# Queries, r and k of five steps as three products of high and low parts, with the buffers and the element-wise work that go with them

## The chip, the core and the metric

The kernel runs on one core of a Trainium2 chip. The metric is device time in microseconds (us). Before the change three runs gave 287.93, 290.63 and 290.19 us, so the median is 290.19 us.

## What is computed

The input is x of shape 4 x 1024 x 256, all in float32. Two blocks follow each other, each behind a layer norm and with a residual.

```
a = layernorm(x)
q = a Wq + bq            k = (a Wk + bk) Wc We      v = (a Wv + bv) Wc We      16 heads of 16, 4 key heads
o = causal linear attention with features elu + 1, divided by (q . cumsum k + 1e-6)
x2 = x + layernorm(a + o Wo + bo) * gamma + beta
z = layernorm(x2),  z_prev = z one token earlier
r = sigmoid((mu_r z + (1 - mu_r) z_prev) Wr^T)
k = relu((mu_k z + (1 - mu_k) z_prev) Wk^T)^2
out = x2 + r * (k Wv^T)
```

## The kernel before, in words

The 1024 tokens are cut into 8 chunks of 128. A chunk holds the 4 batches side by side: 512 columns, in two halves of channels. The kernel has no planner. Each of the five engines has its own program, an order written out by hand, and semaphores join them.

The programs are software-pipelined over steps c = 0 to 6 and a finale. A step works on four chunks at once: it finishes the attention of chunk c, prepares chunk n = c + 1 (transposed input aT, keys, values, queries, denominators), applies output projection and layer norm to chunk m = c - 1, and runs the FFN of chunk f = c - 2. Steps 0 and 1 have no FFN (step 1 has m only), steps 2 to 6 have all four, and the finale (c = 7) runs the attention of the last chunk and the FFN of chunks 5, 6 and 7.

The order in a step with an FFN, engine by engine:

- **TensorE (PE)**: transpose z of f (L469), transpose a of n (L368), spread the reciprocals (L415), output projection (L461), scores (L432), keys and values (L375), r of f (`mix_r`, L483), attention outputs (L448, L453), queries of n (`queries`, L381), keys transposed (L389), state increments (L398), scores, k of f (`mix_k`, L476), outputs, denominators (L406), outputs, v of f (`mix_v_parts`, L501 and L505), first scores of n. L381, L476 and L483 take float32 operands. `mix_v_parts` already uses parts: the product A B is A_high B_high + A_high B_low + A_low B_high, where high is a copy in the type float32r and low is the rest. It holds three matmuls where `mix_v` (L491, the finale) holds one of float32.
- **VectorE (DVE)**: mask of scores (L991), statistics of x (L917), two token shifts for r (L1051, xr), residual of m (L1016) with its statistics, mask, keys and values (L939, L940), centring of m (L1026), key features (L944, L947), second residual of m (L1037, it makes x2), division (L1005), mask, first queries (L953), two token shifts for k (L1051, xk), second queries, division, states (L968), running key sums (L962), statistics of x2, mask, division, two low parts of k's activation (L1109), reciprocal, division, two gates (L1064).
- **ScalarE (ACT)**: copies of zT, aT and the reciprocals, `normalise_x` (L777), exponentials of the keys, tanh of r (L812), exponentials of the queries (L731, L733), copies of values and states, relu, square and high copy of k (L801, L803, L711), copies of transposed keys, `normalise_z` (L785). All copies go through a helper on L711.
- **GpSimd (POOL)**: two token differences (L271, dz), scale and bias of the next x (L222, L216, L218, L226), a + bo (L248), 1/sigma of m (L216, L218), x + beta (L255), denominator terms (L263, prod), scale and bias of z (L222 to L226), two output sums (L278).

The prediction gives places in a step relative to S, the start of the z transposes on TensorE (L469). In the step that is shown S is at 137.57 us.

## Time and profile before

| | |
|---|---|
| median of the runs | 290.19 us |
| profiled execution, whole | 290.58 us |
| its span | 288.8 us |
| busy PE / DVE / ACT / POOL | 264.8 / 225.1 / 154.1 / 127.3 us |
| granted TensorE clock, mean | 0.976 of full |
| step with an FFN, S to S | 30.80 us |
| steps 0 and 1 with the start (to S of step 2) | 74.2 us |
| five steps with an FFN | about 156 us |
| finale | about 58 us |

A row of the timeline has the start in us, the time from the first start to the last end of the merged instructions, the engine, the line, the operation, and the count. A bracket at its end has the idle time before it and what ended that. TensorE's share of busy time is the highest, and a step with an FFN shows hardly a gap on it. The other engines show theirs in brackets.

### The profile page before, as it was taken

Reading aid. Unit: us, or ns where it says so; the run is one execution under the profiler, and the core shown is the slowest. Engines: PE = TensorE matmul, PEld = TensorE weight load, DVE = VectorE, ACT = ScalarE, POOL = GpSimd, SP = SyncE. Lnnn points to the kernel's source line nnn. Section 1 sums busy time; section 2 is a strip of 40 time slices with the busy share of each in tenths; the row PEclk is TensorE's granted clock in tenths of the full one; section 3 lists DMA queues with packets and bytes.
Section 4 is the critical chain, followed back from the end, with each engine's and each line's share of the span. In section 5 each row is a group of like instructions: output and inputs, shape, how many; then the busy total and the mean of one; then the engine's idle time right before and its main releaser. Section 6 shows DMA issues by size and latency. Waiting matters only on the chain.

```text
span 288.8 us, 7520 instructions
## 1 busy us (share of the span) xinstructions
PE 264.8 (92%) x2961; PEld 190.6 (66%) x2961; DVE 225.1 (78%) x550; ACT 154.1 (53%) x312; POOL 127.3 (44%) x151
## 2 busy tenths in 40 slices
PE   7886988983899999999999999999999999989794
PEld 6755656742685588757885588558855767766563
DVE  6587487969597979977997989796979758977523
ACT  2384684480643866388456854586248630453540
POOL 2628423100983358515853576355543514051510
PEclk9998999996599999999999999999999999999999
DMA  7900120000020003000400020001000020000312
GB/s 195 265 19 11 65 76 3 2 0 2 4 72 0 2 24 123 2 5 2 145 2 2 0 76 2 0 2 64 13 2 3 1 74 2 0 2 1 109 36 73
DMA packets 12178, 10.73 MB, mean 37 GB/s; under 512 B 2288, under 2 KB 12144, under 8 KB 12144
## 3 DMA queue, kind: packets, MB, share of 16 engines
q1 hardware_dynamic: 11392, 9.97, 11.1%
q8 instruction: 23, 0.38, 0.5%
q10 hardware_dynamic: 752, 0.30, 0.4%
q14 instruction: 11, 0.09, 0.1%
HBM read 6.07 MB, written 4.19 MB: 36 GB/s over the span
## 4 chain that ended last, share of the span: by engine, by line
PE 77%; DVE 11%; ACT 5%; issue 3%; DMA 2%; POOL 1%; ACTq 0%; DVEq 0%; POOLq 0%
PE ps_x L461 10%; PE ps_x L381 9%; PE ps_z L432 6%; PE ps_x L476 6%; PE ps_x L483 6%; PE ps_x L375 6%; PE ps_y L448 5%; PE ps_y L453 5%; PE ps_x L501 4%; PE ps_x L469 3%; PE ps_z L476 3%; PE ps_z L483 2%; DVE probs L991 2%; PE ps_x L368 2%; PE ps_z L415 2%
## 5 line engine op out<-in xcount | busy, mean ns | idle before, releaser
L991 DVE TENSOR_TENSOR probs<-ps_z,causal 128x1024 f32<-128x1024 f32 x32 | 38.7, 1211 | 6.3 <-PE ps_z L432 5.5
L461 PE MATMUL ps_x<-wo_sb,oT 128*128 128x256 f32 x128 | 29.6, 382 | 0.0
L381 PE MATMUL ps_x<-aT,wq_sb 128*128 128x512 f32 x60 | 27.8, 604 | 0.0
L278 POOL TENSOR_TENSOR out_tok<-tanh_r,x_tok 128x512 f32<-128x512 f32 x14 | 17.8, 1275 | 21.9 <-DVE tanh_r L1064 20.9
L461 PEld LDWEIGHTS ps_x<-wo_sb,oT 128*128 128x128 f32 x128 | 23.6, 190 | 3.8 <-issue 0.9
L248 POOL TENSOR_TENSOR abo_tok<-a_tok,bo_bc 128x1024 f32<-128x1024 f32 x8 | 18.9, 2361 | 16.3 <-issue 5.6
L255 POOL TENSOR_TENSOR xb_tok<-x_in,beta_bc 128x1024 f32<-128x1024 f32 x8 | 18.9, 2356 | 16.0 <-DVE x_tok L1037 16.0
L218 POOL TENSOR_TENSOR rstd<-rstd,neg_half 128x4 f32<-128x4 f32 x24 | 24.9, 1038 | 1.9
L448 PE MATMUL ps_y<-qf,state 32*32 32x128 f32 x512 | 20.9, 278 | 5.3 <-DVE oT L1005 4.7
L432 PE MATMUL ps_z<-qf,kfT 32*128 32x128 f32 x512 | 24.1, 304 | 1.4 <-ACT rden_bc L711 0.5
L263 POOL TENSOR_TENSOR prod<-qf,ksum 128x1024 f32<-128x1024 f32 x5 | 11.8, 2361 | 29.9 <-DVE ksum L962 29.9
L448 PEld LDWEIGHTS ps_y<-qf,state 32*32 32x32 f32 x512 | 12.1, 106 | 19.4 <-issue 11.7
L953 DVE SCALAR_TENSOR_TENSOR qf<-ps_x,bq,eq 128x512 f32<-128x512 f32 x15 | 11.2, 748 | 15.0 <-ACT eq L733 15.0
L432 PEld LDWEIGHTS ps_z<-qf,kfT 32*128 32x128 f32 x512 | 17.9, 191 | 7.4 <-issue 5.0
L222 POOL TENSOR_TENSOR neg_mean<-mv,neg_one 128x4 f32<-128x4 f32 x16 | 5.0, 312 | 38.7 <-DVE mv L923 38.7
L785 ACT ACTIVATE z_tok<-x_tok,nbias,rstd 128x256 f32<-128x256 f32 x32 | 16.6, 591 | 10.2 <-POOL nbias L226 10.2
L1064 DVE SCALAR_TENSOR_TENSOR tanh_r<-tanh_r,ps_x 128x512 f32<-128x512 f32 x13 | 8.9, 686 | 16.5 <-PE ps_x L491 6.5
L453 PE MATMUL ps_y<-probs,v_pad 128*32 128x128 f32 x512 | 21.1, 283 | 0.0
L731 ACT ACTIVATE eq<-ps_x,neg_bq 128x512 f32<-128x512 f32 x15 | 10.3, 687 | 19.9 <-PE ps_x L381 19.9
L777 ACT ACTIVATE a_tok<-x_in,nbias,rstd 128x256 f32<-128x256 f32 x24 | 12.4, 589 | 11.7 <-issue 11.7
L476 PE MATMUL ps_x<-xk,wkT 128*128 128x512 f32 x40 | 18.5, 605 | 0.0
L381 PEld LDWEIGHTS ps_x<-aT,wq_sb 128*128 128x128 f32 x60 | 10.8, 190 | 11.4 <-issue 10.5
(144 smaller groups left out, 623.6 us busy)
## 6 DMA issues: line engine op xcount, KB each, us to landing
x_in<-in_L_attn_x_dram SPq DMA_DIRECT2D x8, 512.0 KB, 4.2
out_dram<-out_tok SPq DMA_DIRECT2D x16, 256.0 KB, 2.1
xr<-in_L_attn_Wq_dram ACTq DMA_DIRECT2D x1, 256.0 KB, 4.0
xk<-in_L_ffn_W_r_dram SPq DMA_DIRECT2D x1, 256.0 KB, 4.8
xk<-in_L_ffn_W_k_dram SPq DMA_DIRECT2D x1, 256.0 KB, 5.0
xr<-in_L_ffn_W_v_dram SPq DMA_DIRECT2D x1, 256.0 KB, 5.5
wo_sb<-in_L_attn_Wo_dram SPq DMA_DIRECT2D x4, 64.0 KB, 5.0
bo_bc<-in_L_attn_bo_dram SPq DMA_DIRECT2D x1, 128.0 KB, 5.0
```

What stands on the lines that cost most here:

```text
L218: PL.tensor_tensor(dst[:], dst[:], neg_half[:], ALU.pow).then_inc(done, 1)
L248: PL.tensor_tensor(abo_tok[n % 2][:], a_tok[n % 2][:], bo_bc[:].unsqueeze(1).to_broadcast([P, NB, D]), ALU.add).then_inc(s_ab, 1)
L255: PL.tensor_tensor(xb_tok[n % 2][:], x_in[n % XBUF][:], beta_bc[:].unsqueeze(1).to_broadcast([P, NB, D]), ALU.add).then_inc(s_xb, 1)
L278: PL.tensor_tensor(out_tok[:, 2 * i:2 * i + 2, :], tanh_r[:, i].rearrange("p (b d) -> p b d", b=2), x2_tok[m % 3][:, 2 * i:2 * i + 2, :], ...
L381: last = mm(bk_[:, :], wq_sb[:, k, a, :], aT[:, k, :], start=(k == 0), stop=(k == KD - 1))
L432: last = mm(ps_z[:, g, u * P:(u + 1) * P], kfT[c % 2][rows, 2 * b + u, :, :], qf[c % 2][rows, :, t0:t0 + HALF], start=True, stop=True, ski ...
L448: mm(ps_y[rows, off + u * P:off + (u + 1) * P], state[rows, slot, b, :, :], qf[c % 2][rows, :, t0:t0 + HALF], start=(u == 0), stop=False, ...
L453: last = mm(ps_y[32 * g:32 * g + 32, off + u * P:off + (u + 1) * P], v_pad[c % 2][:, b, u, g, :, :], probs[b % 2][:, g, u * P:(u + 1) * P] ...
L461: last = mm(bk_[:, (b % 2) * D:(b % 2 + 1) * D], oT[m % 2][:, a, b, :], wo_sb[:, a, :], start=(a == 0), stop=(a == 1))
L476: last = mm(bk_[:, :], wkT[:, k, n * P:(n + 1) * P], xk[:, k, :, :], start=(k == 0), stop=(k == KD - 1))
L483: last = mm(bk_[:, (b % 2) * D:(b % 2 + 1) * D], xr[:, k, b, :], wrT[:, k, :], start=(k == 0), stop=(k == KD - 1))
L991: V.tensor_tensor(probs[b % 2][:].rearrange("p g (r s) -> p g r s", s=HALF), ps_z[:, :, 0:2 * P].rearrange("p g (r s) -> p g r s", s=HALF) ...
```

## The change

**Three products instead of float32.** In steps 2 to 6 the queries, r and k are computed from parts as v already was (`query_parts`, `mix_r_parts`, `mix_k_parts`). In the finale r and v are too, and k stays float32. High parts are copies on ScalarE, low parts are subtractions on GpSimd, both 128x512: six of each in a step, for xr, aT and xk. xr and xk share one pair of buffers, `shift_high` and `shift_low`. The weights Wq, Wr and Wk are split once, in step 0.

**Buffers shared.** z_tok lies in a_tok, prod in eq, wrT and wvT in y_tok. This brings waits with it.

**The shorter steps.** In step 1 the centring and second residual of chunk 0 go from VectorE to ScalarE (`normalise_y`, four of 128x256) and GpSimd (`scale_residual`, eight of 128x256). The denominator terms of steps 0 and 1 go from VectorE to GpSimd, and TensorE takes the denominators behind the last outputs there.

**Order.** In steps 2 to 6 VectorE shifts for k before the first queries. In the finale VectorE makes the second residual of the last chunk behind the shifts for r of the one before it, and GpSimd makes three pairs of low parts for r and three for v.

The program of GpSimd for one step with an FFN (c = 3), first as it was (`dz` to `out_tok`; `mv` and `rstd` are those of x, of y and of z in this order):

```order
L271 TENSOR_TENSOR dz<-zT 128x512 x2
L222 TENSOR_TENSOR neg_mean<-mv,neg_one 128x4
L226 TENSOR_TENSOR nbias<-neg_mean,rstd 128x4
L248 TENSOR_TENSOR abo_tok<-a_tok,bo_bc 128x1024
L216 TENSOR_TENSOR rstd<-mv,ln_eps 128x4
L218 TENSOR_TENSOR rstd<-rstd,neg_half 128x4
L255 TENSOR_TENSOR xb_tok<-x_in,beta_bc 128x1024
L263 TENSOR_TENSOR prod<-qf,ksum 128x1024
```

and as it is with the change (where the denominator terms are written into `eq`):

```order
L292 TENSOR_TENSOR dz<-zT 128x512 x2
L233 TENSOR_TENSOR neg_mean<-mv,neg_one 128x4
L237 TENSOR_TENSOR nbias<-neg_mean,rstd 128x4
L305 TENSOR_TENSOR shift_low<-xr,shift_high 128x512 x2
L227 TENSOR_TENSOR rstd<-mv,ln_eps 128x4
L229 TENSOR_TENSOR rstd<-rstd,neg_half 128x4
L269 TENSOR_TENSOR abo_tok<-a_tok,bo_bc 128x1024
L305 TENSOR_TENSOR aT_low<-aT,aT_high 128x512 x2
L276 TENSOR_TENSOR xb_tok<-x_in,beta_bc 128x1024
L305 TENSOR_TENSOR shift_low<-xk,shift_high 128x512 x2
L284 TENSOR_TENSOR eq<-qf,ksum 128x1024
```

Six subtractions came in, and a + bo went behind 1/sigma of m. The sum x + beta, as before, needs x2 from VectorE.

ScalarE around the queries of the same step, with the change. The first `eq<-ps_x,neg_bq` is the first half of the queries, and `k_act` is the FFN's k:

```order
L831 ACTIVATE eq<-ps_x,neg_bq 128x512 [waits den_ps,qf_ready,q_ps]
L833 ACTIVATE eq<-eq 128x512 [waits negq]
L810 ACTIVATE shift_high<-xk 128x512 [waits xk_ready,r_ps]
L831 ACTIVATE eq<-ps_x,neg_bq 128x512 [waits den_ps,qf_ready,q_ps]
L833 ACTIVATE eq<-eq 128x512 [waits negq]
L810 ACTIVATE shift_high<-xk 128x512 [waits xk_ready]
L810 ACTIVATE v_pad<-v_half 64x4x4x16 [waits o_ps,kv_ready]
L810 ACTIVATE v_pad<-v_half 64x4x4x16 x3
L810 ACTIVATE state<-tail,row_mask 128x4x16 [waits tail_ready]
L810 ACTIVATE state<-tail,row_mask 128x4x16 x3
L908 ACTIVATE k_act<-ps_x 128x512 [waits v_ps,k_ps]
```

The two `shift_high` copies are new here, each of them ahead of work of the queries or the values, and each waits for a token shift of VectorE.

The core of the diff:

```diff
+            def low_parts(parts, whole, high, value, done):
+                for k in range(KD):
+                    pool.wait_ge(high, value + k + 1)
+                    PL.tensor_tensor(flat(parts[1])[:, k * T:(k + 1) * T], whole(k),
+                                     flat(parts[0])[:, k * T:(k + 1) * T].bitcast(F32), ALU.subtract).then_inc(done, 1)
...
+            def query_parts(n, a, bk_):
+                pe.wait_ge(s_aTh, 2 * n - 4)
+                for k in range(KD):
+                    for part in range(2):
+                        mm(bk_[:, :], wq_p[part][:, k, a, :], aT_p[0][:, k, :], start=(k == 0 and part == 0), stop=False)
+                pe.wait_ge(s_aTl, 2 * n - 4)
+                for k in range(KD):
+                    last = mm(bk_[:, :], wq_p[0][:, k, a, :], aT_p[1][:, k, :], start=False, stop=(k == KD - 1))
+                last.then_inc(s_q_ps, 1)
...
             def finale(c):
                 m, f = c - 1, c - 2
                 token_difference(f)
                 first_norm(m)
+                pool.wait_ge(s_k_ps, 2 * f)
+                low_xr(f)
                 second_norm(m)
+                low_ka(f)
                 first_norm(c)
                 token_difference(m)
+                low_xr(m)
                 second_norm(c)
+                low_ka(m)
                 finish(f)
+                low_xr(c)
                 finish(m)
+                low_ka(c)
...
+            def high_part(parts, whole, ready, value, done, ks=range(KD)):
+                for k in ks:
+                    act.wait_ge(ready, value + k + 1)
+                    copy(flat(parts[0])[:, k * T:(k + 1) * T], whole(k)).then_inc(done, 1)
...
                 divide(c, 0)
                 mask(c, 2)
-                queries(n, 0, x0)
                 token_shift(f, 0, *for_k)
                 token_shift(f, 1, *for_k)
+                queries(n, 0, x0)
                 queries(n, 1, x1)
...
                 queries(n, 0, x0)
+                if m >= 0:
+                    second_stats(m, (0, 1))
                 queries(n, 1, x1)
                 divide(c, 1)
                 states(n)
                 key_sums(n)
-                denominator_terms(n)
                 mask(c, 3)
-                if m >= 0:
-                    centre(m)
-                    second_residual(m)
                 divide(c, 2)
```

## Rows read from the trace of the kernel before

**Rows 1.** Busy by stretch of time: PE, PEld, DVE, ACT, POOL, PEclk, DMA share, GB/s.
```profile
65.50:70.00 4.50, 0.62 (x16) 0.35 (x16) 4.50 (x11) 0.00 (x0) 0.00 (x0) 0.75 0.01 4
70.00:78.20 8.20, 7.20 (x77) 5.09 (x77) 5.96 (x22) 3.85 (x8) 6.28 (x7) 0.51 0.00 0
137.57:168.70 31.13, 31.01 (x371) 22.41 (x368) 27.20 (x68) 19.38 (x39) 17.14 (x19) 1.00 0.11 35
```

**Rows 2.** Timeline of PE in one step with an FFN.
```profile
137.57 1.09 PE L469 MATMUL ps_x<-ident,z_tok 128*128 128x128 f32 x8
146.36 3.62 PE L483 MATMUL ps_x<-wrT,xr 128*128 128x256 f32 x16
151.71 3.70 PE L381 MATMUL ps_x<-aT,wq_sb 128*128 128x512 f32 x8
158.11 3.70 PE L476 MATMUL ps_x<-xk,wkT 128*128 128x512 f32 x8
164.65 0.39 PE L501 MATMUL ps_x<-wv_high,ka_high 128*128 128x256 f32 x1
...
167.72 0.73 PE L432 MATMUL ps_z<-qf,kfT 32*128 32x128 f32 x16
168.37 1.09 PE L469 MATMUL ps_x<-ident,z_tok 128*128 128x128 f32 x8
```

**Rows 3.** Timeline of POOL in the same step, and its one subtraction of this form.
```profile
139.33 2.04 POOL L271 TENSOR_TENSOR dz<-zT 128x512 f32<-128x512 f32 x2 [0.19 <-ACT zT L711]
141.32 0.65 POOL L222 TENSOR_TENSOR neg_mean<-mv,neg_one 128x4 f32<-128x4 f32 x1
143.81 0.20 POOL L226 TENSOR_TENSOR nbias<-neg_mean,rstd 128x4 f32<-128x4 f32 x1
144.75 2.37 POOL L248 TENSOR_TENSOR abo_tok<-a_tok,bo_bc 128x1024 f32<-128x1024 f32 x1 [0.75 <-ACT a_tok L777]
147.36 1.02 POOL L218 TENSOR_TENSOR rstd<-rstd,neg_half 128x4 f32<-128x4 f32 x1
151.57 2.35 POOL L255 TENSOR_TENSOR xb_tok<-x_in,beta_bc 128x1024 f32<-128x1024 f32 x1 [3.19 <-DVE x_tok L1037]
...
43.44 1.27 POOL L303 TENSOR_TENSOR wv_low<-wvT,wv_high 128x512 fp32r<-128x512 f32 x1 [5.63 <-ACT wv_high L711]
```

**Rows 4.** Timeline of DVE in the same step.
```profile
140.71 1.87 DVE L1051 SCALAR_TENSOR_TENSOR xr<-dz,mu_r_col,zT 128x512 f32<-128x512 f32 x2
147.50 1.66 DVE L1026 SCALAR_TENSOR_TENSOR y_tok<-y_tok,mv,gamma_bc 128x256 f32<-128x256 f32 x4
149.82 1.67 DVE L1037 SCALAR_TENSOR_TENSOR x_tok<-y_tok,rstd,xb_tok 128x256 f32<-128x256 f32 x4
155.11 0.75 DVE L953 SCALAR_TENSOR_TENSOR qf<-ps_x,bq,eq 128x512 f32<-128x512 f32 x1 [1.92 <-ACT eq L733]
155.78 1.41 DVE L1051 SCALAR_TENSOR_TENSOR xk<-dz,mu_k_col,zT 128x512 f32<-128x512 f32 x2
```

**Rows 5.** Timeline of ACT in the same step.
```profile
153.73 0.69 ACT L731 ACTIVATE eq<-ps_x,neg_bq 128x512 f32<-128x512 f32 x1 [2.89 <-PE ps_x L381]
161.43 0.63 ACT L711 ACTIVATE ka_high<-k_act 128x512 fp32r<-128x512 f32 x1
```

**Rows 6.** Durations of the shifts for r by line, ns min/median/max, in the whole run.
```profile
L1051 DVE SCALAR_TENSOR_TENSOR xr<-dz,mu_r_col,zT x16: 737/743/1511, 79.1 to 275.2; 128x512 f32<-128x512 f32 x16
```

**Rows 7.** Timeline of PE and DVE in step 1.
```profile
66.38 1.66 DVE L1026 SCALAR_TENSOR_TENSOR y_tok<-y_tok,mv,gamma_bc 128x256 f32<-128x256 f32 x4
70.02 1.08 PE L448 MATMUL ps_y<-qf,state 32*32 32x128 f32 x16 [3.90 <-DVE oT L1005]
```

**Rows 8.** Timeline of POOL and PE in the finale.
```profile
253.59 0.20 POOL L226 TENSOR_TENSOR nbias<-neg_mean,rstd 128x4 f32<-128x4 f32 x1
267.12 0.20 POOL L226 TENSOR_TENSOR nbias<-neg_mean,rstd 128x4 f32<-128x4 f32 x1
269.13 1.04 PE L469 MATMUL ps_x<-ident,z_tok 128*128 128x128 f32 x8
```

More of the change, by code:

```diff
@@ L103, in build @@
         s_kd = sem("kf_doubled")
+        wq_p, wr_p, wk_p = ([ctx.enter_context(nc.sbuf_tensor(f"{name}_{part}", [P, *shape], F32R)) for part in ("high", "low")]
+                               for name, shape in (("wq", (KD, 2, P)), ("wr", (KD, D)), ("wk", (KD, D))))
+        wq_split, wr_split, wk_split = sem("wq_split"), sem("wr_split"), sem("wk_split")
+        aT_p, shift_p = ([ctx.enter_context(nc.sbuf_tensor(f"{name}_{part}", [P, KD, T], F32R)) for part in ("high", "low")]
+                         for name in ("aT", "shift"))
+        xr_p = xk_p = shift_p
+        s_aTh, s_aTl, s_xrh, s_xrl, s_xkh, s_xkl = (
+            sem("aT_high"), sem("aT_low"), sem("xr_high"), sem("xr_low"), sem("xk_high"), sem("xk_low"))
         s_kah, s_kal, wv_split = sem("kact_high"), sem("kact_low"), sem("wv_split")
-        y_tok, z_tok = sb("y_tok", NB, D), sb("z_tok", NB, D)
+        y_tok, z_tok = sb("y_tok", NB, D), a_tok
+        wrT, wvT = view(y_tok, 0, KD, D), view(y_tok, KD * D, KD, D)
         stats1, mv1, rstd1 = sb("stats1", NB, 6), sb("mv1", NB, 2), sb("rstd1", NB)
+        neg_mean1, nbias1 = sb("neg_mean1", NB), sb("nbias1", NB)
+        s_nb1, s_n1 = sem("nbias1_ready"), sem("y_scaled")
         stats2, mv2, rstd2, neg_mean2, nbias2 = sb("stats2", NB, 6), sb("mv2", NB, 2), sb("rstd2", NB), sb("neg_mean2", NB), sb("nbias2", NB)
@@ L237, in first_norm, with scale_residual @@
                 rstd(rstd1, mv1, s_rs1, 2 * m + 1)
+            def scale_residual(m):
+                for b in range(NB + 1):
+                    if b < NB:
+                        pool.wait_ge(s_n1, b + 1)
+                        PL.tensor_tensor(y_tok[:, b, :], y_tok[:, b, :], gamma_bc[:], ALU.mult).then_inc(s_t, 1)
+                    if b:
+                        pool.wait_ge(s_t, b)
+                        PL.tensor_tensor(x2_tok[m % 3][:, b - 1, :], y_tok[:, b - 1, :], xb_tok[m % 2][:, b - 1, :],
+                                         ALU.add).then_inc(s_x2, 1)
             def second_norm(m):
@@ L382, in queries, with mix_k_parts, mix_r_parts @@
                 last.then_inc(s_q_ps, 1)
+            def query_parts(n, a, bk_):
[7 more added lines that the diff above has]
+                last.then_inc(s_q_ps, 1)
+            def mix_k_parts(m, n, bk_):
+                cols = slice(n * P, (n + 1) * P)
+                for k in range(KD):
+                    pe.wait_ge(s_xkh, 2 * m + k + 1)
+                    for part in range(2):
+                        mm(bk_[:, :], wk_p[part][:, k, cols], xk_p[0][:, k, :], start=(k == 0 and part == 0), stop=False)
+                for k in range(KD):
+                    pe.wait_ge(s_xkl, 2 * m + k + 1)
+                    last = mm(bk_[:, :], wk_p[0][:, k, cols], xk_p[1][:, k, :], start=False, stop=(k == KD - 1))
+                last.then_inc(s_k_ps, 1)
+            def mix_r_parts(m, i, bk_):
+                pe.wait_ge(s_xrh, 2 * m + 2)
+                for b in (2 * i, 2 * i + 1):
+                    out = bk_[:, (b % 2) * D:(b % 2 + 1) * D]
+                    for k in range(KD):
+                        for part in range(2):
+                            mm(out, xr_p[0][:, k, b * P:(b + 1) * P], wr_p[part][:, k, :], start=(k == 0 and part == 0), stop=False)
+                    if b == 0:
+                        pe.wait_ge(s_xrl, 2 * m + 2)
+                    for k in range(KD):
+                        last = mm(out, xr_p[1][:, k, b * P:(b + 1) * P], wr_p[0][:, k, :], start=False, stop=(k == KD - 1))
+                last.then_inc(s_r_ps, 1)
             def keys_transposed(n):
@@ L485, in mix_r @@
                 last.then_inc(s_r_ps, 1)
-            def mix_v(m, i, bk_):
-                pe.wait_ge(s_ka, 2 * m + 2)
-                for b in (2 * i, 2 * i + 1):
-                    for k in range(KD):
-                        last = mm(bk_[:, (b % 2) * D:(b % 2 + 1) * D], k_act[:, k, b * P:(b + 1) * P], wvT[:, k, :],
-                                  start=(k == 0), stop=(k == KD - 1))
-                last.then_inc(s_v_ps, 1)
             def mix_v_parts(m, i, bk_):
@@ L553, in step @@
                     pe.wait_ge(ffn_w_sb, 1)
-                queries(n, 1, x1)
+                if f >= 0:
+                    query_parts(n, 1, x1)
+                else:
+                    queries(n, 1, x1)
                 outputs(c, 1)
@@ L577, in step @@
                         ffn_weight(2, x1)
-                denominators(n)
+                if f >= 0:
+                    denominators(n)
                 outputs(c, 3)
+                if f < 0:
+                    denominators(n)
                 if f >= 0:
@@ L1087, in step @@
                 mask(c, 2)
-                queries(n, 0, x0)
                 token_shift(f, 0, *for_k)
                 token_shift(f, 1, *for_k)
+                queries(n, 0, x0)
                 queries(n, 1, x1)
```

163 lines of the change are left out of this document (114 added, 49 removed).

## The prediction

> **What bounds the kernel now.** I read the busy time by stretch first, then TensorE's timeline of one step with an FFN, then those of the other engines in that step, then the two ends. In the step from 137.57 to 168.37 TensorE is busy for 31.01 of 31.13 us at full clock, VectorE for 27.20, ScalarE for 19.38, GpSimd for 17.14 [rows 1]. S to S is 30.80 us [rows 2], and TensorE sets it. The reader is to see that VectorE, too, has only some 3.5 us to spare, and that the margins of the other two depend on where their waits lie. GpSimd's long operations stand between VectorE's operations with two inputs in SBUF, hardly ever beside them: a + bo runs from S+7.18 to S+9.55, the centring begins at S+9.93, x2 is done at S+13.92, x + beta begins at S+14.00 [rows 3, 4].
>
> **What TensorE saves.** r takes from 146.36 to about 149.91, 3.55 us for 16 float32 matmuls of 256 columns. v in parts takes 164.65 to 167.72, 3.07 us for 24 [rows 2]. So r saves 0.5. For 512 columns no row shows a matmul of parts. Twice the time of 256 columns is 0.25 us, and that is a bound from above, 3.0 us for the twelve; at the 2.4 GHz of this stretch one column a cycle gives 0.21, 2.6 us, as the lower end. I take 2.8 us against about 3.63 for the float32 form [rows 2]: 0.85 each for queries and k. The sum is 2.2 us a step, and TensorE's own work falls to 28.6 us. That is a gain only if nothing comes later than TensorE does.
>
> **GpSimd's new chain.** A subtraction of 128x512 took 1.27 us and two in a row cost about 2.45 [rows 3]. From dz at S+1.76 the engine is busy up to nbias, which ends at S+6.44 [rows 3]. Then come xr's low parts (to 8.9), 1/sigma of m (1.02 and the 0.3 ahead of it, to 10.25), a + bo (2.37, to 12.65), aT's low parts (to 15.1). r wants xr's low parts at S+9.3: just in time. The queries on TensorE began at S+14.14 [rows 2] and would now begin 0.5 earlier, but the last two products of the first half wait for S+15.1. That half is then done at 15.55 instead of 15.95. ScalarE started on it at S+16.16 after 2.89 us idle [rows 5] and gets it 0.4 earlier. The six high copies there cost 0.63 each [rows 5]; two of them stand ahead of work on the path (one before the second half of the queries, one before the values) and take up ScalarE's slack up to k's relu. TensorE reaches the denominators 1 us early and waits for that relu. So even with no interference a step goes from 30.80 to about 30.35, not to 28.6.
>
> **The shared port.** This is the term that decides. In the step shown the first shift for r starts at 140.71 while dz still runs (to 141.37). The two shifts take 1.87 us there and 1.41 for k, with GpSimd idle [rows 4]: 0.46 more. The line's durations are 743 ns in the middle and 1511 at most [rows 6]. GpSimd in turn takes 0.65 us for a neg_mean of 128x4 while xr runs, where 0.20 is normal for such a size (nbias) [rows 3]. So one of the two engines waits for the other, VectorE until about 0.2 us before the end of GpSimd's operation, and GpSimd gets in between two operations of VectorE. The Trainium skill states this as a rule (SBUF — State Buffer, Who interferes with whom): a VectorE instruction with two SBUF inputs and a GpSimd instruction that reads SBUF exclude each other for the whole instruction. By that rule, the trace agrees (0.46 us), the change is priced by the 307 us below; without it, it would be 290.
>
> Now a + bo arrives at S+10.3, in the middle of the four centrings (from 9.93). It gets in after one or two and holds the others for 2.1 us. The two low parts of aT follow at once and get in between the rest, the key features and the second residual, for 1.1 us each. x2 is then done at S+17.6 to 18.0 and not 13.9. x + beta follows it at once for 2.35 us [rows 3], and now the shifts for k (1.41) stand where VectorE idled for 1.92 us [rows 4]; they wait for it for another 0.6. The second queries, right behind the shifts at S+19.5 before, come at 22.5 to 23.1. k on TensorE waits for them; k's relu, the denominators, v and the next S hang behind. Bounds of the step: below -0.45 us (no interference), above +3.6 (VectorE loses at each meeting). I take +3.0, near the upper end, because the only meeting that the trace shows was lost in full. Five steps: **+15.0 us**.
>
> **The short steps.** In step 0 GpSimd makes the denominator terms. For 1024 columns it takes 2.37 us (a + bo) where VectorE took 1.66 in four pieces [rows 3, 4], but VectorE's next mask is relieved; between 0 and 0.7 later I take **0.4 us**. In step 1 centring (1.66 us [rows 7]) and second residual (as long, by rows 4) leave VectorE; they stood ahead of the division for which TensorE waited 3.90 us, after which the clock was low (0.51 from 70.0 to 78.2) [rows 1, 7]. In their place come four scalings on ScalarE (0.63 at most, what 512 columns take [rows 5]) and eight operations on GpSimd (0.6 each, a quarter of 2.37). By my estimate they end 4 us ahead of that division, beside other work. TensorE still waits for the last mask and for z, some 2 us and 1 us by my estimate. I put z's transposes 4.6 us earlier and take 0.4 back from the low clock: **-5.0 us**; ends -3.5 (the clock falls all the same) and -6.5 (it doesn't).
>
> **The finale.** Six products in parts save 0.3 us each, off the path. GpSimd gets twelve subtractions. v of chunk 5 needs its low parts, which come behind the second norm of chunk 6 (nbias ends at 253.79 [rows 8]): 256.3, so the transposes of z behind it are 2.1 later. The second residual of chunk 7 goes behind two shifts: +1.4. The norm of chunk 7 ended at 267.32 [rows 8], now 270.8; v of chunk 6 waits for the low parts behind it, 273.3, and z's transposes behind that start at 274.4 instead of 269.13 [rows 8]: +5.3. At the end v's low parts stand behind an output sum: +0.7. That is +6.0 without the port, +8 if both second residuals meet xr's low parts. I take **+6.5 us**; the lower end is 0, if v's first half finds its parts ready.
>
> **Other edits.** wq, wr and wk are split in step 0 beside waits of ScalarE and GpSimd: 0. Shared buffers cost only waits that are long fulfilled: a_tok for z (its a + bo ends on GpSimd at S+12.7, z is written at the step's end), eq (the denominators of the chunk before), one pair for xr and xk (r ends at S+11.9, xk's copy comes at S+17 or later): 0. No DMA is moved; loads wait for x + beta, which comes up to 4 us later, a whole step ahead of need.
>
> **The sum.** 290.6 (the profiled execution) + 0.4 - 5.0 + 15.0 + 6.5 = 307.5. The profiled execution is 0.4 above the median, so **307 us** is the forecast.
>
> **Rivals.**
>
> - *The port costs little, and the chain over GpSimd and ScalarE sets the step.* For it: only short meetings are in the trace. Against: they were lost in full. 290.6 + 0.4 - 5.0 - 5 x 0.45 + 6.0 = 289.8, **290 us**. Chance 0.20: 0.06 faster, 0.10 same, 0.04 slower.
> - *TensorE stays the bound: faster.* The place is the first half of the queries. If aT's low parts are there by S+14.5 (GpSimd ready 0.6 earlier and no loss at the port) and ScalarE's two copies fit into its idle time, TensorE never waits, and the finale costs nothing net: 290.6 - 5 x 2.2 - 5.0 = **275 us**. For it: TensorE is the bound in the busy shares, and ScalarE idles for 11.8 us a step [rows 1]. Against: GpSimd's chain adds up to 15.1. Chance 0.16.
> - *Half the blocking.* VectorE loses one long operation, not three: +1.2 us a step, 298 us. Chance 0.10, slower.
> - *The forecast*, with the port lost in full or nearly: 0.54, slower. Its own range is 300 to 314, from +2.2 to +3.6 a step and the ends of the finale. If TensorE's waits also lower its clock, as after the wait in step 1, it is above that.
>
> **Range.** 286 to 314 leaves out the second rival, the fastest part of the first, and a clock that falls in the steps: about 0.2. A change within 1% (2.9 us) can't be told from none. Faster 0.06 + 0.16 = 0.22, same 0.10, slower 0.04 + 0.10 + 0.54 = 0.68.
>
> **What would show it.** Twelve matmuls of 512 columns at 0.21 to 0.25 us apart show TensorE's term. The port: the four centrings longer than 1.66 us in sum, one of them at 2 us or more, and VectorE's second residual ending near S+17.8. The chain: idle time of TensorE before the matmuls of k, and S to S near 33.8. The finale: waits of TensorE for the low parts of v. The prediction is wrong if the centrings stay at 0.48 us each beside a running a + bo, or if S to S falls below 30.

## The result

Times are device microseconds, medians; the ratio is that of the undisturbed runs with its 95% interval.

| | before | after |
|---|---|---|
| median | 290.22 (287.93 to 290.63, 4 runs) | 317.17 (313.45 to 318.91, 4 runs) |
| ratio to before | | 1.085 (1.075 to 1.094) |
| span and mean clock of the profiled run | 288.8, 0.976 | 311.7, 0.962 |

The kernel got slower, as forecast (307 us), but by more than the range (to 314) held. Two of the four runs after the change, 318.77 and 318.91, had a lower mean clock (0.935); the ratio and all that follows rest on the others, 313.45 and 315.58, so "the changed kernel" below is 314.5 us. The profiled execution, 313.45, lies just inside the range, and 314.5 just outside it.

Where it went, by the two profiled executions (S is the first transpose of z in a step, as in [rows 2]):

| stretch | before | after | difference | forecast |
|---|---|---|---|---|
| start, steps 0 and 1, to S of step 2 | 74.26 | 67.09 | -7.2 | -4.6 |
| five steps with an FFN | 155.7 | 174.0 | +18.3 | +15.0 |
| finale, to the end | 58.8 | 70.6 | +11.8 | +6.5 |

The view by stretch of the changed kernel (columns as in [rows 1]): start and short steps, then three of the five steps, then the finale.

```profile
0.00:67.09 67.09, 55.93 (x773) 40.40 (x774) 48.39 (x134) 41.38 (x87) 42.88 (x65) 1.00 0.25 69
136.27:170.32 34.05, 29.37 (x384) 23.36 (x381) 31.84 (x67) 22.33 (x45) 24.92 (x24) 1.00 0.11 32
170.32:206.30 35.98, 31.98 (x384) 25.61 (x381) 31.86 (x67) 22.56 (x45) 24.88 (x24) 0.91 0.05 16
206.30:241.09 34.79, 30.82 (x384) 24.64 (x380) 30.24 (x58) 20.37 (x40) 22.39 (x20) 0.95 0.05 17
241.09:311.70 70.61, 51.59 (x420) 40.00 (x416) 42.16 (x87) 26.54 (x51) 32.02 (x34) 0.90 0.09 31
```

Beside the last line of [rows 1] the second line tells most. TensorE is busy for 29.4 us where it was 31.0 (in a window 0.3 us longer), so the parts do save there. VectorE is busy for 31.8 where it was 27.2, without one operation more in this stretch: its operations have become longer. VectorE is now the busiest engine of the step. The third and fourth lines have the same work at a lower clock and are 1.9 and 0.7 us longer.

The step that begins at 136.27, on VectorE and then on GpSimd (timelines, columns as in [rows 3, 4]):

```profile
146.20 5.83 DVE L1165 SCALAR_TENSOR_TENSOR y_tok<-y_tok,mv,gamma_bc 128x256 f32<-128x256 f32 x4
152.68 1.67 DVE L1176 SCALAR_TENSOR_TENSOR x_tok<-y_tok,rstd,xb_tok 128x256 f32<-128x256 f32 x4
155.74 2.26 DVE L1191 SCALAR_TENSOR_TENSOR xk<-dz,mu_k_col,zT 128x512 f32<-128x512 f32 x2
159.34 0.75 DVE L1091 SCALAR_TENSOR_TENSOR qf<-ps_x,bq,eq 128x512 f32<-128x512 f32 x1 [0.68 <-ACT eq L833]
```

```profile
146.39 2.52 POOL L269 TENSOR_TENSOR abo_tok<-a_tok,bo_bc 128x1024 f32<-128x1024 f32 x1
148.88 2.87 POOL L305 TENSOR_TENSOR aT_low<-aT,aT_high 128x512 fp32r<-128x512 f32 x2
154.43 2.36 POOL L276 TENSOR_TENSOR xb_tok<-x_in,beta_bc 128x1024 f32<-128x1024 f32 x1 [2.68 <-DVE x_tok L1176]
```

The four centrings took 1.66 us in [rows 4]; now 5.83, from 146.20 to 152.0, and beside them GpSimd runs from 146.39 to 151.75. x2 is done at S+18.1 where it was S+13.9. The shifts for k, 1.41 us before, run beside x + beta and take 2.26. The second query comes at S+23.1. Over the whole run the line of the centrings has a median of 1488 ns where a lone one takes 470:

```profile
L1165 DVE SCALAR_TENSOR_TENSOR y_tok<-y_tok,mv,gamma_bc x28: 471/1488/2710, 77.9 to 270.4; 128x256 f32<-128x256 f32 x28
```

TensorE in the same step, its waits in brackets:

```profile
151.80 0.73 PE L452 MATMUL ps_x<-aT_low,wq_high 128*128 128x512 f32 x2 [0.79 <-POOL aT_low L305]
154.74 0.64 PE L543 MATMUL ps_y<-qf,state 32*32 32x128 f32 x16 [0.82 <-DVE oT L1141]
158.81 0.46 PE L493 MATMUL ps_x<-v_half,kf 128*32 128x32 f32 x32 [2.27 <-DVE qf L1091]
160.14 0.50 PE L460 MATMUL ps_x<-shift_high,wk_high 128*128 128x512 f32 x1 [0.22 <-DVE qf L1091]
160.48 0.40 PE L460 MATMUL ps_x<-shift_high,wk_low 128*128 128x512 f32 x1
160.72 0.39 PE L460 MATMUL ps_x<-shift_high,wk_high 128*128 128x512 f32 x1
...
163.10 0.64 PE L543 MATMUL ps_y<-qf,state 32*32 32x128 f32 x16
```

Before there was hardly a wait. k takes 160.14 to 163.10, 2.96 us for twelve matmuls 0.23 to 0.24 apart, against 3.70 [rows 2].

The finale on VectorE, GpSimd and TensorE:

```profile
259.44 3.71 DVE L1176 SCALAR_TENSOR_TENSOR x_tok<-y_tok,rstd,xb_tok 128x256 f32<-128x256 f32 x4
277.89 3.71 DVE L1176 SCALAR_TENSOR_TENSOR x_tok<-y_tok,rstd,xb_tok 128x256 f32<-128x256 f32 x4
```

```profile
259.78 2.69 POOL L305 TENSOR_TENSOR shift_low<-xr,shift_high 128x512 fp32r<-128x512 f32 x2 [4.08 <-ACT shift_high L810]
266.74 0.20 POOL L237 TENSOR_TENSOR nbias<-neg_mean,rstd 128x4 f32<-128x4 f32 x1
266.89 2.50 POOL L305 TENSOR_TENSOR ka_low<-k_act,ka_high 128x512 fp32r<-128x512 f32 x2
278.18 2.73 POOL L305 TENSOR_TENSOR shift_low<-xr,shift_high 128x512 fp32r<-128x512 f32 x2 [3.53 <-ACT shift_high L810]
285.18 0.20 POOL L237 TENSOR_TENSOR nbias<-neg_mean,rstd 128x4 f32<-128x4 f32 x1
```

```profile
269.44 0.51 PE L592 MATMUL ps_x<-wv_high,ka_low 128*128 128x256 f32 x2 [3.79 <-POOL ka_low L305]
270.50 1.55 PE L564 MATMUL ps_x<-ident,a_tok 128*128 128x128 f32 x8
287.88 0.76 PE L592 MATMUL ps_x<-wv_high,ka_low 128*128 128x256 f32 x2 [3.78 <-POOL ka_low L305]
289.72 1.84 PE L564 MATMUL ps_x<-ident,a_tok 128*128 128x128 f32 x8
303.82 0.50 PE L592 MATMUL ps_x<-wv_high,ka_low 128*128 128x256 f32 x2 [1.83 <-POOL ka_low L305]
```

The finale begins at 229.97 before and 241.09 after. From there the norms of chunks 6 and 7 end at +23.8 and +37.4 in [rows 8] and at +25.9 and +44.3 here; z's last transposes, at +39.2 in [rows 8], are at +48.6. Both second residuals (1.67 and 1.66 us before) take 3.71, each beside xr's low parts, and v waits three times for low parts. Two more things show here. The centrings of chunk 7 take 2.59 us (1.70 before), beside the first low parts of the key activations. And the granted clock, 1.00 in the whole finale before, is 0.90 in its mean and 0.71 in its last 11.7 us.

### The profile page after: what moved, and what is told of

It is laid out like the page before. It is cut to its first block, busy times and chain, and to the rows that moved or that the text cites. A ratio compares the mean times of both kernels' runs of the same rounds, so it can differ in the third digit from the quotient of the medians.

```text
span 311.7 us, 7915 instructions
## 1 busy us (share of the span) xinstructions
PE 259.1 (83%) x3089; PEld 200.7 (64%) x3089; DVE 248.4 (80%) x540; ACT 179.3 (58%) x361; POOL 196.9 (63%) x208
## 4 chain that ended last, share of the span: by engine, by line
DVE 42%; PE 24%; issue 11%; POOL 11%; ACT 9%; DMA 1%; POOLq 1%; DVEq 0%; ACTq 0%
DVE y_tok L1165 10%; DVE stats L1055 5%; DVE probs L1127 5%; DVE x_tok L1176 4%; PE ps_x L588 3%; DVE xk L1191 3%; DVE xr L1191 3%; PE ps_x L556 3%; PE ps_x L442 2%; PE ps_y L543 2%; PE ps_y L548 2%; DVE y_tok L1155 2%; PE ps_x L592 2%; POOL rstd L229 2%; POOL out_tok L299 2%
## 5 line engine op out<-in xcount | busy, mean ns | idle before, releaser
L1165 DVE SCALAR_TENSOR_TENSOR y_tok<-y_tok,mv,gamma_bc 128x256 f32<-128x256 f32 x28 | 33.3, 1247 | 0.0
L305 POOL TENSOR_TENSOR shift_low<-xr,shift_high 128x512 fp32r<-128x512 f32 x16 | 20.5, 1304 | 15.0 <-ACT shift_high L810 15.0
L527 PE MATMUL ps_z<-qf,kfT 32*128 32x128 f32 x512 | 23.8, 300 | 1.9 <-ACT rden_bc L810 0.5
L269 POOL TENSOR_TENSOR abo_tok<-a_tok,bo_bc 128x1024 f32<-128x1024 f32 x8 | 19.4, 2430 | 8.7 <-issue 5.2
L1204 DVE SCALAR_TENSOR_TENSOR tanh_r<-tanh_r,ps_x 128x512 f32<-128x512 f32 x13 | 8.9, 686 | 19.7 <-PE ps_x L592 19.4
L527 PEld LDWEIGHTS ps_z<-qf,kfT 32*128 32x128 f32 x512 | 17.6, 189 | 7.8 <-issue 4.7
L892 ACT ACTIVATE a_tok<-x_tok,nbias,rstd 128x256 f32<-128x256 f32 x32 | 16.6, 591 | 7.4 <-POOL nbias L237 7.4
L810 ACT ACTIVATE shift_high<-xr 128x512 fp32r<-128x512 f32 x16 | 9.9, 631 | 18.8 <-DVE xr L1191 18.8
L292 POOL TENSOR_TENSOR dz<-zT 128x512 f32<-128x512 f32 x14 | 14.3, 1042 | 9.6 <-ACT zT L810 9.6
L284 POOL TENSOR_TENSOR eq<-qf,ksum 128x1024 f32<-128x1024 f32 x7 | 16.7, 2385 | 5.1 <-DVE ksum L1100 5.0
L810 ACT ACTIVATE kf<-kf 128x256 f32<-128x256 f32 x7 | 2.9, 415 | 28.1 <-DVE kf L1085 28.1
L592 PE MATMUL ps_x<-wv_high,ka_low 128*128 128x256 f32 x52 | 11.2, 299 | 9.4 <-POOL ka_low L305 9.4
L305 POOL TENSOR_TENSOR shift_low<-xk,shift_high 128x512 fp32r<-128x512 f32 x10 | 12.9, 1285 | 9.2 <-ACT shift_high L810 9.2
```

The lines of the kernel that those rows point to most:

```text
L269: PL.tensor_tensor(abo_tok[n % 2][:], a_tok[n % 2][:], bo_bc[:].unsqueeze(1).to_broadcast([P, NB, D]), ALU.add).then_inc(s_ab, 1)
L305: PL.tensor_tensor(flat(parts[1])[:, k * T:(k + 1) * T], whole(k), flat(parts[0])[:, k * T:(k + 1) * T].bitcast(F32), ALU.subtract).then_i ...
L527: last = mm(ps_z[:, g, u * P:(u + 1) * P], kfT[c % 2][rows, 2 * b + u, :, :], qf[c % 2][rows, :, t0:t0 + HALF], start=True, stop=True, ski ...
L1165: V.scalar_tensor_tensor(out=y_tok[:, b, :], in0=y_tok[:, b, :], scalar=mv1[:, b, 0:1], in1=gamma_bc[:], op0=ALU.subtract, op1=ALU.mult).t ...
```

## The experiments

The kernels of one group ran on the same chip beside the kernel before (288.8 to 290.3 us). The steps are S to S for steps 2 to 5, at the clock that each had; "centrings" is the sum of the four in the step whose length is in bold. A time is the median of a kernel's runs, and for the changed kernel the 314.5 us from above.

| kernel | time | ratio to before | S of step 2 | steps 2 to 5 | centrings |
|---|---|---|---|---|---|
| before | 290.2 | | 74.26 | 32.51, 30.80, **30.80**, 30.80 | 1.66 |
| changed | 314.5 | 1.085 (1.075 to 1.094) | 67.09 | 35.04, 34.14, **34.05**, 35.98 | 5.83 |
| short_alone | 283.9 | 0.979 (0.974 to 0.984) | 66.98 | 31.44, 30.80, 30.79, 30.80 | |
| q_float32 | 304.1 | 1.050 (1.045 to 1.056) | 67.51 | 33.95, 33.01, **32.02**, 33.01 | 3.79 |
| writes_only | 294.7 | 1.016 (1.011 to 1.022) | 68.84 | 31.10, 30.68, 30.60, **30.60** | 1.67 |
| finale_in_float32 | 303.1 | 1.047 (1.040 to 1.054) | 67.33 | 35.42, 34.54, 34.07, 34.05 | |
| filled_waits | 312.0 | 1.076 (1.071 to 1.081) | 67.32 | 34.77, 34.12, 34.06, 34.07 | |
| bo_late | 314.3 | 1.086 (1.079 to 1.093) | 67.58 | 35.34, 34.38, 34.88, **31.96** | 3.72 |
| r_in_float32 | 313.8 | 1.086 (1.083 to 1.090) | 67.08 | 35.03, 34.27, **35.77**, 34.72 | 5.51 |
| combined | 286.1 | 0.987 (0.983 to 0.992) | 68.28 | 31.74, 31.09, 31.10, **31.10** | 1.66 |
| a_bo_in_gap | 280.2 | 0.968 (0.964 to 0.971) | 67.56 | 32.03, 29.96, **29.96**, 29.97 | 1.66 |
| only_queries | 280.1 | 0.970 (0.966 to 0.975) | 70.43 | 30.68, 30.10, 30.10, 30.10 | |
| start_filled | 279.5 | 0.964 (0.961 to 0.968) | 70.26 | 30.69, 29.97, 29.96, 29.96 | |
| finale_writes | 309.7 | 1.070 (1.065 to 1.075) | 67.57 | 35.98, 34.73, 34.56, 34.08 | |

**The short steps alone** (short_alone). The kernel before, with these edits of the change and no parts but those of v:

```diff
-                centre(m)                    # VectorE, step 1
-                second_residual(m)
-                denominator_terms(n)         # VectorE, steps 0 and 1
...
+                normalise_y(m)               # ScalarE, step 1
+                scale_residual(m)            # GpSimd, step 1
+                denominator_terms(n)         # GpSimd, steps 0 and 1
```

> The kernel before with the changes of steps 0 and 1 alone (scaling and residual of chunk 0 on ScalarE and GpSimd, denominator terms on GpSimd, denominators behind the last outputs in steps 0 and 1); five steps and finale as before. Prediction's own terms: +0.4 - 5.0, so 290.6 to 286.0, start to S of step 2 69.7 us. Rival, from the trace of the changed kernel (67.09 there): the rest of the change does not touch this stretch, 283.2 to 283.5 in all, and the clock of the stretch is 1.00. If the 67.09 came from a clock that happened to be high in that one execution, 286 to 290 and the clock falls to about 0.5 near 70 us.

The rival held for the stretch: S of step 2 is at 66.98, where the changed kernel has 67.09, so the rest of the change does not touch it. The time, 283.9 us, is 0.4 above the rival's upper end. The clock of the stretch in the profiled execution:

```profile
0.00:66.98 66.98, 56.21 (x774) 40.69 (x774) 48.37 (x134) 39.91 (x84) 39.10 (x62) 1.00 0.25 69
```

By the traces the term was -7.3 and not -4.6; by the medians (283.9 against 290.2) it was -6.3. In [rows 1] and [rows 7] a wait of 3.90 us is followed by a stretch at clock 0.51; in the changed kernel TensorE waits 1.88 us at the same place and the clock stays. In the traces that came out better than the end of the estimate that had it stay (-6.5).

**Queries in float32** (q_float32). No high and low parts of aT:

```diff
-                    low_parts(aT_p, lambda k: aT[:, k, :], s_aTh, 2 * n - 6, s_aTl)
...
-                    query_parts(n, 0, x0)
+                    queries(n, 0, x0)
```

> The changed kernel with float32 queries in the five steps: no high and low parts of aT. TensorE has 0.85 us more of its own work a step. Port theory: of GpSimd's three long operations that meet VectorE's centrings, a + bo stays and two of 1.1 us go: the centrings take 3.5 to 4.0 us in sum and not 5.83, x2 is done 1.8 us or more earlier, S to S is 31.5 to 32.5 and the time 303 to 308. Rival (the chain over ScalarE's copies and the low parts of xr and xk sets the step): centrings shorter, S to S unchanged at 34. Rival (TensorE's own time counts): S to S gets longer by up to 0.85 us, 318.

The port theory held in each number: centrings 3.79 us, x2 done at S+16.0 and not 18.1, the step at full clock 32.02, 304.1 us. TensorE has about 0.7 us more to do in a step (3.70 against 2.96 us, as for k), and the step is 2.0 us shorter. Together with the steps at lower clock, the queries' parts cost the changed kernel 10 us.

**Fills in place of subtractions** (writes_only). a + bo and aT's low parts become writes of the same length:

```diff
+                    link(PL.memset(scratch[:], 0.0))
+                    PL.memset(flat(parts[1])[:, k * T:(k + 1) * T].bitcast(F32), 0.0).then_inc(done, 1)
...
+                for _ in range(2):
+                    link(PL.memset(scratch[:], 0.0))
+                PL.memset(abo_tok[n % 2][:], 0.0).then_inc(s_ab, 1)
...
-                    add_bo(n)
+                    write_bo(n)
...
-                    low_parts(aT_p, lambda k: aT[:, k, :], s_aTh, 2 * n - 6, s_aTl)
+                    low_writes(aT_p, s_aTh, 2 * n - 6, s_aTl)
```

> The changed kernel with a + bo and the low parts of aT on GpSimd replaced, in the five steps, by plain fills of about the same duration, which write SBUF and read nothing (this leaves out that part of the computation). All waits and the order stay. If VectorE is held off by GpSimd's reads, the four centrings take 1.66 us in sum, as before the change, x2 is done near S+14 and S to S is 31 to 32, the time 300 to 305. If any long work of GpSimd, or any write of it, holds VectorE off, the centrings stay at 5.8 us and S to S at 34. If GpSimd's chain by its own length sets the step, the centrings fall and S to S stays at 34.

In the step from 161.22, VectorE and then GpSimd:

```profile
171.16 1.67 DVE L1180 SCALAR_TENSOR_TENSOR y_tok<-y_tok,mv,gamma_bc 128x256 f32<-128x256 f32 x4
172.74 0.94 DVE L1097 TENSOR_SCALAR ek<-ek 128x256 f32<-128x256 f32 x1
174.14 1.67 DVE L1191 SCALAR_TENSOR_TENSOR x_tok<-y_tok,rstd,xb_tok 128x256 f32<-128x256 f32 x4
```

```profile
171.31 1.22 POOL L314 MEMSET scratch<- 128x576 f32 x2
172.59 0.95 POOL L315 MEMSET abo_tok<- 128x1024 f32 x1
173.48 0.72 POOL L306 MEMSET scratch<- 128x576 f32 x1
174.26 0.53 POOL L307 MEMSET aT_low<- 128x512 f32 x1
```

GpSimd writes from 171.31 without a pause, and the centrings take 1.67 us. So what holds the centrings off is neither GpSimd's being busy nor its writes, but its reads. The mechanism came as expected; the gain was underestimated. The step is 30.60 us (31 to 32 expected) and the time 294.7 (300 to 305): 20 us of the changed kernel's time hang on the reads of these three operations of each step, stretches at lower clock included. So 30.60 is near what the change would give without this loss; the shifts for k still met x + beta (2.31 us, 1.41 before). The chain worked out for that case gave 30.35.

The Trainium skill (SBUF — State Buffer, Who interferes with whom) says of a VectorE instruction with two SBUF inputs that it contends with a GpSimd instruction that reads SBUF, not with one that only writes it. The trace agrees: 5.83 us beside reads, 1.67 beside writes.

**The finale in float32** (finale_in_float32):

```diff
-                low_xr(f)
                 second_norm(m)
-                low_ka(f)
                 first_norm(c)
...
-                mix_v_parts(f, 0, x1)
+                mix_v(f, 0, x1)
```

> The changed kernel with r and v of the last three chunks in float32, as in the kernel before: no low parts of xr and of the key activations on GpSimd in the finale, the second residual of chunk 7 ahead of the shifts (float32 v weights are summed up again from their two parts in step 6). Prediction's term for the finale is +6.5: 314.5 would become 308. The two traces say +11.8: if all of it hangs on GpSimd's low parts, the granted clock's low stretches among it, the time is 302 to 303 and the finale takes 58.8 us again; if the low clock of the finale has another cause, the time is 305 or more and the clock of the finale stays at about 0.9.

303.1 us, 11.4 less than the changed kernel. From z's transposes of chunk 5 to those of 6, and on to those of 7, it takes 19.4 and 13.7 us, as before the change (the changed kernel: 23.4 and 19.2). The finale as a whole:

```profile
239.46:300.70 61.24, 52.33 (x385) 37.09 (x384) 38.36 (x87) 19.61 (x39) 17.23 (x22) 0.96 0.11 35
```

That is 61.2 us, not the 58.8 expected. So 9.4 of the finale's 11.8 us hang on the low parts. Of the other 2.4 some 0.7 lie ahead of z's transposes of chunk 5, and 1.7 behind those of chunk 7, in part of which the clock is down (0.83 from 280 to 290 us) though no low parts are left there; what brought it down is open. The five steps, which this edit doesn't touch, are 1.9 us shorter in this execution than in the changed kernel's, so a part of the 11.4 us is not the finale's. (A first form of this kernel, finale_float32, kept Wr, Wk and Wv in SBUF as float32 beside their parts. It doesn't fit there and has no time.)

**Fills in the finale** (finale_writes): xr's low parts there as fills, the key activations' as they are.

```diff
-                low_parts(xr_p, lambda k: xr[:, k].rearrange("p b t -> p (b t)"), s_xrh, 2 * m, s_xrl)
+                for k in range(KD):
+                    pool.wait_ge(s_xrh, 2 * m + k + 1)
+                    link(PL.memset(scratch[:], 0.0))
+                    PL.memset(flat(xr_p[1])[:, k * T:(k + 1) * T].bitcast(F32), 0.0).then_inc(s_xrl, 1)
```

> The changed kernel with xr's low parts of the finale (three chunks, two each) replaced on GpSimd by plain fills of the same duration, which read nothing (this leaves out that part of the computation). The low parts of the key activations and all waits stay. Of the +11.8 us of the finale, the port's share: both second residuals take 1.67 us and not 3.71, z's transposes of chunk 6 come 2.0 us earlier and those of chunk 7 4.1 us earlier, time 309.5 to 311. If VectorE's waits there come from elsewhere, the second residuals stay at 3.71 and the time at 313 to 315. The rest of the +11.8, some 7 us, is then GpSimd's chain: the key activations' low parts behind the norms and the output sums.

309.7 us, 4.8 less, as expected. The two second residuals of the finale:

```profile
261.09 1.67 DVE L1180 SCALAR_TENSOR_TENSOR x_tok<-y_tok,rstd,xb_tok 128x256 f32<-128x256 f32 x4
...
277.53 1.67 DVE L1180 SCALAR_TENSOR_TENSOR x_tok<-y_tok,rstd,xb_tok 128x256 f32<-128x256 f32 x4
```

Counted from those of chunk 5, z's transposes come 1.9 and 4.8 us earlier than in the changed kernel, and the end comes 5.7 us earlier. So 4.8 (by the medians) to 5.7 us (by the traces) of the 11.8 are xr's reads beside VectorE. The other 6 to 7 us are GpSimd's chain and what comes with it: the centrings of chunk 7 still take 2.59 us, and the clock is at 0.84 and 0.85 from 270 to 290 us. The runs don't part these.

**Filled waits** (filled_waits). Nine products of the identity with itself in TensorE's wait of 2.27 us:

```diff
+                if f >= 0:
+                    pe.wait_ge(s_pr, 8 * c + 6)
+                    fill(9)
                 state_increments(n)
```

> The changed kernel with nine products of the identity with itself put where TensorE waits 2.3 us before the state increments of the five steps. No other engine gets anything. If the half clock behind this wait in steps 5 and 6 (+1.9 and +0.7 us) comes from the wait, all steps take 34.05 us at clock 1.00, and the time is 2 to 3 us below that of the changed kernel, about 312. If the clock falls for another reason, nothing changes or the step gets longer by what the fillers take beyond the wait: 314 to 316.

Behind the first, steps 3 to 5 took 34.12 us at most, and the time was 312.0. The step that took 35.98 at 0.91 in the changed kernel:

```profile
170.27:204.34 34.07, 31.38 (x402) 25.44 (x399) 31.87 (x67) 22.32 (x45) 24.91 (x24) 1.00 0.06 18
```

This is what the theory expected. It isn't proof: in finale_in_float32, which has the same wait of 2.3 us, and in bo_late (1.9 to 2.3), single steps ran at full clock too, and others did not. And the intervals of this kernel (1.071 to 1.081) and of the changed one (1.075 to 1.094) overlap.

**a + bo late** (bo_late): GpSimd makes it behind the second norm.

```diff
-                    add_bo(n)
                     low_parts(aT_p, ...)
...
                     second_norm(m)
+                    add_bo(n)
```

> The changed kernel with GpSimd's a + bo behind the second norm in the five steps, not ahead of aT's low parts. The same operations, none left out. Port theory: the centrings meet two operations of 1.25 us and not one of 2.4 and one or two of 1.25: 3.5 to 4 us in sum and not 5.83; aT's low parts are ready 2.4 us earlier, so the first queries do not wait. x2 is done 2 us or more earlier, S to S 31.5 to 32.5, time 303 to 307. Rival (the sum of GpSimd's work sets the step, wherever it stands): S to S stays at 34, or gets longer where the work moved meets the low parts of the key activations.

A miss in the time. The centrings fell to 3.72 us, x2 was done at S+16.0, and the one step at full clock took 31.96 us: all as expected. But in four of the five steps the clock was down for a part (0.90 to 0.95), and a + bo now met the low parts of the key activations, which took 2.65 us together in the step from 137.30 where they take 0.7 each alone. In these four steps TensorE waited 0.7 to 1.6 us for these low parts, and in the one at full clock it didn't. The time stayed at 314.3. So the second half of the rival came true, "gets longer where the work moved meets the low parts of the key activations", and its first half did not: at full clock, where the meeting was short, the place counted for 2.1 us of a step.

**r in float32** (r_in_float32):

```diff
-                    low_parts(xr_p, ..., s_xrh, 2 * f, s_xrl)
                     first_norm(m)
                     add_bo(n)
...
-                    mix_r_parts(f, 0, x1)
+                    mix_r(f, 0, x1)
```

> The changed kernel with r of the five steps in float32 (the finale as changed). GpSimd's chain is 2.5 us shorter ahead of a + bo, which then runs from about S+7.6 to S+10.1, mostly ahead of the centrings; aT's low parts (1.25 us each) meet them. Port theory: centrings 3.5 to 4.2 us in sum and not 5.83, S to S 31.5 to 32.5 for 0.5 us more of TensorE's work, time 303 to 308 with the low clock that comes with TensorE's waits. Rival (what counts is the number of GpSimd's operations and not where they lie): S to S 33.5 or more, 312 or more.

A miss. xr's low parts had been hardly a link of the chain: without them GpSimd waited 1.89 us for the statistics of the first norm, and a + bo began at S+9.6 instead of S+10.1. The centrings took 5.51 us, 313.8 us in all. The rival's number came, and its reason (the number of operations) didn't: the place had not moved.

**Parts without meetings** (combined, then a_bo_in_gap). Queries and k in parts, r and the finale in float32, and GpSimd's order in a step (short names, not the source):

```diff
-  dz, norm_x, low(xr), first_norm, add_bo, low(aT), add_beta, low(xk), terms, second_norm
+  dz, norm_x, low(aT), first_norm, low(xk), add_bo, terms, second_norm, add_beta    # combined
+  dz, norm_x, low(aT), first_norm, add_bo (behind x2), low(xk), terms, ...          # a_bo_in_gap
```

> The short steps of the change, queries and k of the five steps in three products of parts, r and the whole finale in float32; GpSimd's order in a step: dz, norm of x, aT's low parts, first norm, xk's low parts, a + bo, denominator terms, second norm, x + beta behind the low parts of the key activations. So nothing long on GpSimd stands beside the centrings, the second residual or the shifts. Port theory: centrings 1.66 us and xk's shifts 1.41 us in sum, TensorE's 1.7 us of savings a step come through in part: S to S 29.3 to 30.3, time 276 to 282. Rival (VectorE with 27 of 30 us, or ScalarE's copies, set the step now): S to S 30.6 to 30.8 as without the change, 283 to 284. Rival (moved work delays the denominators or the loads): over 31, 285 or more.

The centrings took 1.66 us, x2 was done at S+13.9, but the step took 31.10. TensorE's only wait was for the denominator terms, behind a + bo on GpSimd. First TensorE's timeline, then GpSimd's:

```profile
187.86 0.64 PE L477 MATMUL ps_x<-eq,head_cols 128*32 128x128 f32 x16 [1.58 <-POOL eq L283]
```

```profile
180.05 1.28 POOL L304 TENSOR_TENSOR shift_low<-xk,shift_high 128x512 fp32r<-128x512 f32 x1 [7.65 <-ACT shift_high L792]
182.99 2.40 POOL L268 TENSOR_TENSOR abo_tok<-a_tok,bo_bc 128x1024 f32<-128x1024 f32 x1
185.34 2.38 POOL L283 TENSOR_TENSOR eq<-qf,ksum 128x1024 f32<-128x1024 f32 x1
```

It was the third outcome, "moved work delays the denominators", and the row shows the place for a + bo: the 7.65 us of idle time.

> The combined kernel with GpSimd's a + bo right behind the second residual (it waits for x2) and not between xk's low parts and the denominator terms. In the combined kernel TensorE's only wait of a step, 1.58 us, was for these terms, which started 1.4 us late behind a + bo. GpSimd idled for 7.65 us ahead of xk's low parts. Theory: the wait goes, a + bo meets at most the first shift for k (up to 0.6 us, of which VectorE's later waits of 0.28 and 1.01 us take most): S to S 31.10 - 1.58 + 0.3 = 29.5 to 29.9, time 278 to 281. Rival (VectorE or ScalarE sets the step, the wait only moves): 30.5 to 31, 283 to 286.

280.2 us, 3.2% faster than before, 11% faster than the changed kernel. Beside the short steps alone (ratio 0.979, 30.80 us a step) the parts of queries and k bring 1.1%, some 3 us in all. S to S is 29.96, 0.06 above what was expected. a + bo meets a shift for k (2.06 us for the two, not 1.40).

**Only the queries** (only_queries): the same with `mix_k` for `mix_k_parts` and no parts of xk.

> As the kernel with a + bo in the gap, but with k in float32: of the parts in the five steps only the queries' and v's are left. TensorE's own work is 0.85 us a step more. If TensorE is the bound there, S to S is 30.0 to 30.2 and the time 280 to 282 (short steps alone: 283.9); if something else sets the step near 29.5 to 30, there is no difference to the kernel with k in parts.

S to S 30.10 and 280.1 us. k in parts saves 0.14 us a step and nothing that the times can tell. Most of the 0.7 us that it saves on TensorE come back as a wait: 0.5 us a step for ScalarE's `k_act`, where only_queries has no wait that the profile lists.

**Filled waits at the start** (start_filled): the kernel with a + bo in the gap, with seven products ahead of the last outputs of step 1, four ahead of z's first transposes.

> The kernel with a + bo in the gap, with products of the identity with itself in TensorE's two waits at the end of step 1 and the start of step 2: seven where it waits 1.87 us for VectorE's division, four ahead of z's transposes. In the kernel without them the clock was at half for 6.8 us from 65.3 on, and step 2 took 32.03 us where the others take 29.96. If these waits bring the clock down, step 2 takes 30 to 30.4 us at clock 1.00, and the time is 277.5 to 279.5. If not, nothing changes: 280, step 2 at 32.

Inconclusive: the execution that was traced took 283.25 us, the longest of its seven, so its steps say little. In a_bo_in_gap step 2 ran at clock 0.93; here it ran at 1.00, but the stretch ahead of it was at 0.95, by low clock between 20 and 50 us, where nothing had been put, and the sum of both is not shorter (100.95 against 99.59 us):

```profile
0.00:70.26 70.26, 62.57 (x796) 46.14 (x796) 48.39 (x134) 40.98 (x86) 41.28 (x64) 0.95 0.22 66
70.26:100.95 30.69, 30.07 (x373) 23.43 (x372) 27.55 (x66) 22.76 (x47) 22.03 (x21) 1.00 0.06 19
```

Its time, 279.5, can't be told from 280.2 (ratios 0.961 to 0.968 and 0.964 to 0.971).

## Why the prediction was right in its direction and short in its size

- **What bounds the kernel.** TensorE with 31.0 us of a step, VectorE 3.5 us behind: right, and this margin is what the change used up. VectorE was busy for 4.6 us more of a step, with longer operations and not with more of them.
- **TensorE's savings.** Forecast 2.2 us a step; with k at 2.96 us, not 2.8, and the queries the same, it is 2.0. With the loss at the port none of it reached the time; with the fills 0.2 did (30.60), where 0.45 had been forecast.
- **The shared port, five steps at +3.0.** The mechanism is shown: fills in place of reads give the centrings back (1.67 us), and queries in float32 give half of the loss back. At full clock the step is 34.05, +3.25; x2 at S+18.1 (forecast 17.6 to 18.0), second query at S+23.1 (22.5 to 23.1). A detail was off: all three operations of GpSimd fell on the four centrings, and none on the second residual.
- **The clock in the steps.** The forecast said that TensorE's waits might lower it and left it out of sum and range. It cost 1.9 + 0.7 us in steps 5 and 6 of the profiled run. Its link to the wait of 2.27 us is supported by the filled waits (2.5 us less, with overlapping intervals), not settled.
- **The short steps, -4.6.** Measured -7.3 by themselves in the traces (-6.3 in the medians). The wait there halved, and the clock stayed at 1.00. In the other direction than the rest, this hid a part of the miss. That the profiled execution lies inside the range is owed to it, and so is luck.
- **The finale, +6.5: the step that failed.** It came to +11.8. The term that was mis-sized is the port's: it had been put at +0.5, and at +2 at most, "if both second residuals meet xr's low parts". Both did, and fills in place of these low parts gave back 4.8 to 5.7 us. Each second residual lost 2.0 us, both in a row on the same chain. The prediction's own price in the steps, 1.1 us for each low part that gets in, would have given 4.4 for these four. Full loss was assumed in the steps, where one meeting was in the trace, and hardly any in the finale. One rule, priced in two ways in one sum, is the error. The chain without the port had been put at +6.0; 6 to 7 us are left with the fills, but these hold a low clock and lengthened centrings that the term didn't have, so its size isn't shown.
- **The range.** Its upper end is 290.6 + 0.4 - 3.5 + 18.0 + 8.0 = 313.5, with the finale at its own upper end of +8. The finale was 3.8 us above that, and low clock in the steps wasn't in it. The lower end doesn't come out of the terms: +2.2 a step and 0 in the finale give 297 and not 300.
- **The rivals.** "The port costs little" is out by the centrings. "TensorE stays the bound" is out with this order on GpSimd, and a_bo_in_gap shows that its premise was about the order: with r in float32 and nearly all meetings gone the parts bring S to S to 29.96. "Half the blocking" (+1.2 a step) is what q_float32 has at full clock.

The terms add up: -2.6 (start) + 1.3 (steps at full clock) + 2.0 (steps, the rest, mostly clock) + 5.3 (finale) = 6.0 us beyond the forecast, for the profiled execution (313.45 against 307.5).

What stays open: what decides in which step the clock falls (steps with the same wait of 2.3 us ran at 1.00 and at 0.91), and how much of the finale's loss is its low clock.

## What to carry to other kernels

Before moving work to GpSimd, lay its long operations that read SBUF over VectorE's timeline and count each meeting with a queue of operations of two SBUF inputs at what is left of GpSimd's operation, everywhere in the kernel by the same price. Then look for the gaps: a + bo and aT's low parts, moved to where they meet at most one such operation, left the centrings at 1.66 us. With r and the finale back in float32 that turned +8.5% into -3.2%, of which the short steps alone are 2.1%. A saving on the engine that bounds the step is worth only what the next wait leaves of it: here the queries' parts brought 0.70 us of a step (30.80 to 30.10), and k's, as large on TensorE, 0.14.
